# A feed-forward stage with picked tokens: order of its products, index work, weighted sum and row replacement

## What is computed

```
x1 = x @ sw1.T + sb1 ; x2 = x @ sw2.T + sb2                   # shared expert, all 2048 tokens
shared_out = LN(silu(x1) * x2) @ sw3.T + sb3
x_moe = x[index_b, index_t]                                   # 512 picked tokens
scores = sigmoid(x_moe @ eg_w.T + eg_b) ; top1 = argmax(scores + exp_bias)
h1, h2 = 8 experts' products of x_moe ; z = LN(silu(h1) * h2) ; out_all = z @ ew3 + eb3
picked = shared_out[picked] * shared_w + out_all[top1] * expert_w
final = shared_out.at[index_b, index_t].set(picked)           # rows replaced; the last of equal indices wins
x = layernorm(x + final)
```

## Time and profile before

| | us |
|---|---|
| median of 3 runs (3375.1 to 3379.15) | 3375.57 |
| the profiled execution | 3380.29 |
| its span in the trace | 3378.5 |
| index phase, first row of it to first row of the product phase | 472.49 to 512.42 |
| product phase, to first product of the layer norm | 512.42 to 561.66 |
| layer norm of Z, and gate phase, to the first bias product | 561.66 to 614.86 |
| sum phase, to the finish's first product | 614.86 to 651.73 |
| finish, to the store of its rows | 651.73 to 675.71 |
| store, gathers, turning, to the next sublayer's first load | 675.71 to 713.74 |

### The profile page before, as it was taken

How to read it: one execution, slowest core, us unless ns; L and a number is a source line. 1 busy time by engine, 2 the same in 40 slices (tenths; PEclk the granted TensorE clock), 3 DMA queues, 4 the chain that set the end, 5 groups by cost and what they waited for, 6 DMA issues and landing times. The chain is left out here.

```text
span 3378.5 us, 53803 instructions
## 1 busy us (share of the span) xinstructions
PE 2841.4 (84%) x18568; PEld 1727.8 (51%) x18569; DVE 1865.6 (55%) x4547; ACT 1601.3 (47%) x4391; POOL 676.7 (20%) x757
## 2 busy tenths in 40 slices
PE   7788948638999998679979998999988889959992
PEld 4634633414555555346645563355634356639992
DVE  5655763624887885667656642266423648633333
ACT  5335942314777774772235542155421539713331
POOL 3110020112121120012116630066300003201113
PEclk9879979769999999889999999999999989959996
DMA  1010020010000001000010000000000000141112
GB/s 69 2 18 1 2 82 0 7 62 1 2 2 2 2 2 38 25 13 2 17 40 1 1 34 28 6 1 1 1 28 13 6 23 2 37 197 36 36 35 82
DMA packets 35171, 80.64 MB, mean 24 GB/s; under 512 B 8897, under 2 KB 23826, under 8 KB 30834
## 3 DMA queue, kind: packets, MB, share of 16 engines
q1 hardware_dynamic: 30002, 64.68, 5.3%
q0 software_dynamic: 4368, 11.93, 1.2%
q10 hardware_dynamic: 560, 0.93, 0.1%
HBM read 63.18 MB, written 14.02 MB: 23 GB/s over the span
## 5 line engine op out<-in xcount | busy, mean ns | idle before, releaser
L2459 ACT ACTIVATE scores<-scores,min 128x128 f32<-128x128 f32 (+7 forms) x256 | 198.4, 775 | 86.6 <-DVE min L2442 82.8
L2440 DVE TENSOR_SCALAR zero_marks<-psum 128x128 f32<-128x128 f32 (+7 forms) x256 | 192.1, 751 | 67.9 <-PE psum L2372 65.6
L2442 DVE CUSTOM_DVE_ANT_0 scores<-psum,zero_marks 128x128 f32<-128x128 f32 (+7 forms) x256 | 194.0, 758 | 29.9 <-issue 0.9
L2379 PE MATMUL psum<-ident,scores 128*128 128x128 f32 x1152 | 173.1, 277 | 16.8 <-ACT probsT L2476 13.9
L2476 ACT ACTIVATE probsT<-psum 128x128 f32<-128x128 f32 (+7 forms) x256 | 163.0, 637 | 32.9 <-PE psum L2379 32.3
L3783 PE MATMUL psum<-Hn,W 128*128 128x512 f32 x384 | 169.5, 605 | 8.7 <-PEq L415 8.7
L1597 ACT ACTIVATE XT<-psum,b_of_tile 128x128 f32<-128x128 f32 x312 | 89.0, 368 | 178.8 <-PE psum L1517 178.8
L1517 PE MATMUL psum<-x_gatheredT,XT 128*128 128x128 f32 x1248 | 153.3, 283 | 6.1 <-issue 3.2
L1517 PEld LDWEIGHTS psum<-x_gatheredT,XT 128*128 128x128 f32 x1248 | 148.4, 198 | 12.9 <-issue 11.8
L2379 PEld LDWEIGHTS psum<-ident,scores 128*128 128x128 f32 x1152 | 123.4, 141 | 56.3 <-issue 29.9
L2369 PE MATMUL psum<-XT,Q_heads 64*128 64x512 f32 x256 | 143.7, 641 | 0.0
(11 more groups left out here) (623 smaller groups left out, 6756.4 us busy)
## 6 DMA issues: line engine op xcount, KB each, us to landing
W<-in_L3f_W SPq DMA_DIRECT2D x16, 1024.0 KB, 22.4
L3f_y_rows<-y SPq DMA_DIRECT2D x39, 128.0 KB, 1.7
L0f_rows<-Xtok SPq DMA_DIRECT2D x2, 2048.0 KB, 7.7
W<-in_L0f_W SPq DMA_DIRECT2D x3, 1152.0 KB
early_weights<-in_L2f_Wqkv SPq DMA_DIRECT2D x2, 1536.0 KB
W<-in_L2f_W SPq DMA_DIRECT2D x2, 1536.0 KB
XT<-in_xT SPq DMA_DIRECT2D x1, 2048.0 KB, 9.2
Xtok<-in_xtok SPq DMA_DIRECT2D x1, 2048.0 KB
```

The lines of the kernel that those rows point to most:

```text
L2379: ins = pe.transpose(turned[:, kt * P:(kt + 1) * P], Sc[:, i % ROT, kt * P:(kt + 1) * P], K.ident[:])
L2440: dve.tensor_scalar(zero[:, i % 2, 0:n], sc(i)[:, 0:n], 0.0, -NEG, ALU.is_equal, ALU.mult)
L2442: dve.tensor_tensor_reduce(Sc[:, i % ROT, 0:n], sc(i)[:, 0:n], zero[:, i % 2, 0:n], 1.0, -NEG, ALU.add, ALU.min, low[:, i % ROT:i % ROT + ...
L2459: act.activation(p, p, ACT.Exp, bias=low[:, i % ROT:i % ROT + 1], scale=-1.0, accum_out=sums[:, u % 2, h:h + 1]).then_inc(s["exp_done"], 1)
```

## The change

- The DRAM tensor and its semaphore `K.rows_out` are made once in `program`. The finish of the sublayer ahead stores its four blocks of rows as they are done, behind SP's early loads; the shared expert's own weights and the biases b1, b2 (four loads) are loaded there too, into `K.early`.
- Index and product phase are one. Order on PE: units 9..12 (shared expert, all tokens), the turning of the picked tokens, then units 0..8. The `arrive` is gone: PE waits for `K.late` ahead of unit 0. DVE makes the flat index first, and the 16 hit pairs stand between the units' products, with semaphores in place of drains.
- Sum: the four bias products go to four banks with no wait between them; the expert e is the outer loop and q the inner, and there is no drain behind an add: DVE waits by semaphore for the add four before. SP does not wait for the store of `acc`.
- `finish_replaced` takes the place of `finish`, of the store and gathers, and of `turn_tokens`. The bias is a second product of 256 columns on PE (one partition of ones against the bias row); POOL's 16 adds are gone. SP stores each finished pair of tiles; POOL waits for that pair and gathers its two tiles; PE turns tile t - 13 behind product t; DVE and ACT copy tiles in turn, after all statistics and all normalising.

```
 finish(), SP, behind the early loads:
+            if K.rows is not None:
+                for q in range(NT // TPB):
+                    sp.wait_ge(s["tok_done"], TPB * (q + 1))
+                    sp.dma_start(K.rows[q * BLK:(q + 1) * BLK].rearrange("(t p) d -> p t d", p=P), K.Xtok[:, q * TPB:(q + 1) * TPB, :]).then_inc(K.rows_out, 16)
 L0_ffn:
+            order = [n for n in range(NJ) if n > L0E] + [None] + list(range(L0E + 1))
...
-                    sp.dma_start(pool_of_rows[0:TOK].rearrange("(t p) d -> p t d", p=P), K.Xtok[:]).then_inc(s["rows_out"], 16)
...
+                    pe.wait_ge(K.late, shared_in)
+                    for p, n in enumerate(order):
+                        free(p)
+                        if n is None:
+                            pe.wait_ge(s["picked"], 16 * PT4)
...
+                        if p == AT + 1:
+                            pe.wait_ge(K.late, all_in)
+                            pe.wait_ge(s["picked_out"], PT4)
...
+                        while made < min(NT, (i + 1) * NT // (NJ - 1)):
+                            hits(made)
+                            if made:
+                                last_of(made - 1)
+                            made += 1
...
-            arrive(nc, K)
...
-                    if q:
-                        pe.wait_ge(s["bias_out"], q)
-                    pe.matmul(K.bank[1][:, 0:D], gT[:, q * P:(q + 1) * P], b3[:], start=True, stop=True).then_inc(s["bias_done"], 1)
+                    pe.matmul(bias_bank(q)[:, 0:D], gT[:, q * P:(q + 1) * P], b3[:], start=True, stop=True).then_inc(s["bias_done"], 1)
...
-                    q, e = divmod(n, L0E + 1)
+                    e, q = divmod(n, PT4)
                     dve.wait_ge(s["done"], n + 1)
+                    if n >= PT4:
+                        dve.wait_ge(s["added"], n - PT4 + 1)
...
-                sp.wait_ge(s["stored"], 16)
...
+ finish_replaced(), SP and POOL:
+            for p in range(PAIRS):
+                sp.wait_ge(s["tok_done"], 2 * p + 2)
+                sp.dma_start(pool_of_rows[2 * p * P:(2 * p + 2) * P].rearrange("(t p) d -> p t d", p=P), K.Xtok[:, 2 * p:2 * p + 2, :]).then_inc(s[f"stored{p}"], 16)
...
+            pool.wait_ge(K.rows_out, 16 * (NT // TPB + 1))
+            for p in range(PAIRS):
+                pool.wait_ge(s[f"stored{p}"], 16)
+                for t in pair(p):
+                    pool.indirect_dma_start(out=K.Xtok[:, t, :], out_offset=None, in_=pool_of_rows[:, :],
+                                            in_offset=bass.IndirectOffsetOnAxis(ap=home[:, t:t + 1], axis=0)).then_inc(s[f"gathered{p}"], 16)
```

More of the change, by code:

```diff
@@ L2516, in _, with normalise @@
         @block.scalar
         def _(act):
-            for t in range(0, NT, 2):
[L2519 to L2526, removed]
+            def normalise(p):
+                act.wait_ge(s["recip_done"], p + 1)
+                for t in pair(p):
+                    tok = K.Xtok[:, t, :]
+                    act.activation(tok, tok, ACT.Identity, bias=st[:, t, 2:3], scale=st[:, t, 8:9]).then_inc(s["tok_done"], 1)
@@ new lines, in _ @@
+                @block.scalar
+                def _(act):
+                    act.wait_ge(K.late, shared_in)
+                    for p, n in enumerate(order):
+                        if n is None:
+                            for q in range(PT4):
+                                act.wait_ge(s["turned"], q // 2 * 2 + 2)
+                                act.activation(XmT[:, :, q * P:(q + 1) * P], slot(p, q // 2)[:, (q % 2) * D:(q % 2 + 1) * D].rearrange("p (c k) -> p c k", c=2),
+                                               ACT.Copy).then_inc(s["picked_out"], 1)
+                            continue
+                        i = before(p)
+                        act.wait_ge(s["done"], i + 1)
+                        if i >= 2:
+                            act.wait_ge(s["z_done"], i - 1)
+                        act.activation(sl[:, i % 2, :], slot(p, 0), ACT.Silu, bias=b1[:, expert(n):expert(n) + 1]).then_inc(s["silu_done"], 1)
@@ L2605, in _ @@
                     dve.scalar_tensor_tensor(out=fr[:, 0], in0=fr[:, 0], scalar=float(S), in1=fr[:, 1], op0=ALU.mult, op1=ALU.add)
                     dve.drain()
-                    for t in range(NT):
-                        dve.scalar_tensor_tensor(out=hit[:], in0=fr[:, 0], scalar=tok[:, t:t + 1], in1=order[:], op0=ALU.is_equal, op1=ALU.mult)
-                        dve.drain()
-                        dve.reduce_max(last[:, t, 0:1], hit[:], AX)
-                        dve.drain()
-                    dve.tensor_scalar(last[:, :, 1], last[:, :, 0], 0.0, None, ALU.is_gt)
@@ new lines, in _ @@
+                    made = 0
+                    for p, n in enumerate(order):
+                        if n is None:
+                            continue
+                        i = before(p)
+                        dve.wait_ge(s["silu_done"], i + 1)
+                        dve.scalar_tensor_tensor(out=Z[:, n, :], in0=slot(p, 1), scalar=b2[:, expert(n):expert(n) + 1], in1=sl[:, i % 2, :],
+                                                 op0=ALU.add, op1=ALU.mult).then_inc(s["z_done"], 1)
+                        while made < min(NT, (i + 1) * NT // (NJ - 1)):
[3 more added lines that the diff above has]
+                            made += 1
@@ L3854, in program @@
                 K.ahead = early_loads(K, w, after)
+                K.rows = row_pool if after is L0_ffn else None
+                if sublayer is L0_ffn:
+                    K.rows = row_pool
+                    if i == first:
+                        load(nc, K, later=early_loads(K, w, L0_ffn))
+                        store_rows(nc, K)
                 sublayer(nc, K, w)
```

232 lines of the change are left out of this document (151 added, 81 removed).

## The result

The changed kernel takes 3328.68 us (median of 4 runs, 3325.78 to 3331.04); the kernel before, run beside it, took 3377.36 (3375.1 to 3381.42). The ratio is 0.9852, 95% interval 0.9838 to 0.9866. It is faster by 48.7 us where 69.1 were forecast, and lies 7.7 us above the upper end of the range. The profiled execution took 3329.15, with a span of 3327.4.

A forecast was written before the change was run, and what follows sets the result against it. Phases meet between, so what ends last sets each: PE in products, DVE's drained adds late in the sum, then store, gathers and turning in series. Savings 32.6 + 7.3 + 2.5 + 26.7 = 69.1 us off 3375.57 gave 3306.5, range 3298 to 3321.

The forecast's parts named there:

- A: Joint index and product phase: shared units hidden behind the gathers' wait; 32.6 us saved after a clock charge, bounds 25.5 to 35.5.
- the hits were hidden: Rival in the joint phase: DVE's hit pairs aren't hidden, a semaphore wait making each cost 3.2; 14 us lost, 3320, chance 4%.
- The 1.7 charged for the clock: Layer norm after the joint phase: PE idles 3.9 us ahead, not 1.8, so lost clock costs 1.7 us.
- B: Sum phase: bias products without waits and adds without drain take 22.3 us instead of 29.65; 7.3 us saved.
- C: Between sum and finish: no wait for the store of acc; 2.5 us saved.
- D: Finish with replacement: POOL's gathers set the pace, ending at 35.3 us instead of 62.0; 26.7 us saved, bounds 18 to 28.6.
- The rival on the low clock: Sum and finish: PE gaps from bias products and adds keep the clock low throughout; 18.3 us lost, 3324.8, chance 4%.
- gathers beside DVE's statistics: Rival in the finish: DVE's statistics keep POOL's gathers out until 23.0 us; 11.9 us lost, 3318.4, chance 6%.
- stores and gathers didn't take turns: Rival in the finish: stores land only between gathers, so eight pairs go one behind the other; 3352, slower from k = 11.8; 1.5%.

## Why the prediction was right or wrong

**A: right in its sum, 34.7 for 32.6, and in part by luck.** The indices came 6.9 us into the phase, 7.0 forecast, but by two errors that cancel: without the store ahead of them SP issued the last index load 1.7 us in, not 4.6 (470.72 against 469.05), and it then took 5.2 to land, not the 2.5 taken. The shared units ended 1.1 us ahead of the picked rows, 1.0 forecast; the hits were hidden. The experts' start was 0.9 early. The 1.7 charged for the clock is near the 1.1 lost, and its place is wrong: the clock was granted in full for 25 us behind the layer norm's wait (1.00 from 522 to 547), and from its first product to the first of its second pass it is 30.3 us in both kernels. The 1.1 were lost in that second pass (13.12 before, 14.24 after), behind an idle time of 4.3 us that both kernels have. In the run with the ten more products the same wait did cost: the first six instructions took 5.46, not 3.06.

**B and C: right.** 7.0 for 7.3 and 2.4 for 2.5. The 0.3 that B lacks are in the bias products: the four took 3.71 to the first of the 36, where 3.4 were forecast, for their 9 rows are followed by 128. An add without drain keeps up with a product, as the row of another sublayer said.

**D: wrong by 16.0, and all of the miss in the sublayer** (14.4; A to C gave 1.6 more than forecast). The step that failed: "The finish of the first sublayer has the same load on PE, two products a tile, and no POOL add ... and PE's extra bias product fits in." The two products there are both of 128 rows. Here the second has one row. By the runs, two things follow, which the rows that the prediction read don't show:

- A product whose rows differ in number from those of the one ahead leaves its weight load uncovered: 0.29 us at half clock, 0.20 at full (0.625 against 0.43). With 32 products that is 9.3 us at half clock.
- In the alternating finish the clock was never granted in full, and fell where it was full at entry.

The kernel before showed both in other rows of its trace. In its own sum phase the last bias product, of 9 rows, stands 1.14 ahead of the first product of 128 rows, not 0.86:

```profile
620.07 1.22 PE L2737 MATMUL psum<-b,gatesT 9*128 9x256 f32 x2 [0.52 <-DVE acc L2755]
621.21 6.01 PE L2742 MATMUL psum<-W,Z 128*128 128x256 f32 x14
```

And the 32-row products shown above stayed at the low clock for 14 us. So both the uncovered load and a low clock under few rows stood in the trace of before, away from the rows chosen as the analog.

Their sum is D's miss. The rival on the low clock had the finish's tiles end 27.9 us in, at 2 x 0.86 each, and the end at 40.9, 5.6 more than the forecast's 35.3. Measured, the last product ends 37.5 us in (640.49 + 1.22 - 604.23 = 37.48), 9.6 more than that, nearly all of it the uncovered loads, and the end is 13.9 behind it, where that rival had 13.0. So 5.6 + 9.6 + 0.9 = 16.1.

The rival "the low clock stays" thus had a third of D's miss (5.6 of 16.0). That its price, 3324.8, came close to the result is luck: 12.7 of its 18.3 us were in the sum, where none were lost. Its reason was wrong, too: it feared gaps from the bias products and the adds in the sum, where the clock rose (1.00 granted from 587 on); and what it had against itself was again the first sublayer's finish. The other rivals fell: gathers beside DVE's statistics were issued 1.25 apart without gaps with 128 rows, so GpSimd was not held up; the hits were hidden; a pair waited only for its products, so stores and gathers didn't take turns.

The section "Architectural detail" of the page "TensorE: Matmul & The Clock Gate" of the Trainium skill says that TensorE's queue can pull a weight load ahead of products in flight. The loads here agree between products of equal height (0.86 apart at half clock, load and product overlapping) while at each change of height none was pulled ahead: load and product start together. The section names no such case. The section on LDWEIGHTS of the same page of the Trainium skill has the load's time depend on its columns and not on its rows. The rows agree: one row takes 0.50 for two loads, as 128 do.

**What the whole time has beyond the sublayer.** The sublayer saves 54.7 us in the profiled executions, the whole 51.1 there and 48.7 by medians. The rest of the program, which is the same code but for the stores in the finish ahead, takes 3137.3 before and 3140.9 after; over the sixteen profiled executions it ranges from 3130.1 (128 rows) to 3142.4, the same stretch between two loads taking, for instance, 29.5 or 32.9 us, and another 805.7, 809.0 or 812.3. Three us less ahead of the sublayer and 7 more behind it belong to that. So differences of whole times under some 12 us between single executions say nothing of an edit, and I read the stretches. The forecast of the whole time was 22.2 us too low: 14.4 in the sublayer, 6.0 outside it (54.7 against 48.7 by the medians), 1.8 in the kernel before, which took 3377.36 beside the changed one and 3375.57 when the forecast was made. Whether the 6.0 are such scatter or an effect on what follows stays open: no run tells. The 26.4 by which the profiled execution of the 128-row version beats its own are 15.7 in the stretch and 10.7 in the rest, of which I claim the first alone.

## What to carry to other kernels

Look for an analog of each engine's load with the same shapes, rows of the stationary operand included, before saying that an extra product fits in; "two products a tile" was not enough. A bias product of one partition between full ones can cost far more than its arithmetic: here 16 us in 16 tiles, and spreading it over all 128 partitions (a tile of 1/128 against the bias on every partition) gave all of it back, at a cost of at most 1.4. Where products of few rows are needed, keeping them together saves the uncovered loads (11.2 of the 15.7 came back with five and five in turn), but not the clock, which fell again behind each such group.

## What the runs showed of the hardware

- Two products of different height don't overlap load and product: 1.15 us apart instead of 0.86 at half clock, 0.625 instead of 0.43 at full, with 1 row and, at half clock, with 9 and 64 alike.
- TensorE can show as busy for 5.0 of 5 us over 30 us and be granted 0.50 of its clock throughout: one-row or 64-row products alternating with 128-row ones, and, for 14 us, 32-row products alone. With 128-row products alone it rose within 7 us (0.50, 0.81, 1.00 over three stretches of 5); with short one-row products between them it rose as well; with five and five in turn it rose and fell (0.50, 0.81, 0.66).
- Ten products that nobody reads, made while PE would have stood idle, kept the clock full over the wait ahead of the finish, and moved the first gather from 13.2 (616.71 - 603.51) to 10.6 us (614.85 - 604.29) behind the store of acc.
